# Attention on one core: where the sums of probabilities run, and how many buffers they and the outputs have

## The reference, cut to what matters

```python
def xattn(query, key, value, Wq, Wk, Wv, Wo):           # query (16,112,1024), key = value = ctx (16,375,1024)
    q = (query @ Wq).reshape(b, sq, 32, 32).transpose(0, 2, 1, 3)
    k = (key @ Wk).reshape(b, sk, 8, 32).transpose(0, 2, 1, 3)      # v likewise; each serves 4 heads
    scores = einsum('bhqd,bhkd->bhqk', q, k) * 32 ** -0.5
    probs = softmax(scores, axis=-1)
    out = einsum('bhqk,bhkd->bhqd', probs, v)
    return out.transpose(0, 2, 1, 3).reshape(b, sq, 1024) @ Wo
x = x + xattn(layernorm(x), ctx, ctx, Wq, Wk, Wv, Wo)
x = x + ffn(layernorm(x), w1, w1_scale, w3, w3_scale, w2, w2_scale)  # silu(x w1) * (x w3), then w2
```

## Time and profile before

| | |
|---|---|
| median of 3 runs | 2506.35 us (2501.25 to 2508.3) |
| span of the profiled execution | 2511.5 us (the page gives no other time for it) |
| PE busy | 2424.5 us, 97% of the span, 12682 matmul rows |
| DVE, ACT, POOL busy | 1727.6, 979.1 and 576.1 us |
| line 816, sums | 256 rows, median 563 ns, first at 282.8 us, last at 852.1 us |
| line 924, products with values | 768 rows |

### The profile page before, as it was taken

One profiled execution on the slowest core, in us unless ns is written; L12 is line 12 of the kernel. 1 busy time (PEld: TensorE's weight loads), 2 busy tenths in 40 slices (PEclk: granted clock), 3 DMA queues, 4 the chain that ended last, 5 costly groups with the idle time before them and its releaser, 6 DMA issues.

```text
span 2511.5 us, 35414 instructions
## 1 busy us (share of the span) xinstructions
PE 2424.5 (97%) x12682; PEld 2069.3 (82%) x12682; DVE 1727.6 (69%) x2639; ACT 979.1 (39%) x1673; POOL 576.1 (23%) x305
## 2 busy tenths in 40 slices
PE   7998999999999699799999999999999989999999
PEld 7997878878876388699999988998899978888887
DVE  6425777777776446788888889898889874445442
ACT  3212445444454422444444445344443342323221
POOL 1000354454454400011111111332333320000000
PEclk9998999999998799899999999999999999999999
DMA  7534555455545345465655554666676687565652
GB/s 225 174 96 135 146 135 146 131 142 143 133 113 130 86 155 168 126 203 168 186 170 168 165 151 148 181 180 183 194 211 182 172 284 228 170 186 151 186 163 84
DMA packets 369146, 408.04 MB, mean 162 GB/s; under 512 B 125824, under 2 KB 324096, under 8 KB 359152
## 3 DMA queue, kind: packets, MB, share of 16 engines
q1 hardware_dynamic: 369008, 406.22, 56.7%
HBM read 252.99 MB, written 152.70 MB: 162 GB/s over the span
## 4 chain that ended last, share of the span: by engine, by line
PE 44%; DVE 9%; issue 3%; DMA 2%; ACT 0%; DVEq 0%; ACTq 0%
PE bank L84 15%; PE bank L85 15%; PE bank L86 15%; DVE g_WL L90 2%; DMA stash<-weight_scratch 2%; DVE g_su L1731 1%; DVE stash L1736 1%; DVE g_XL L90 1%; DVE stash L1228 1%; DVE stash L1226 1%; DVE xT L1723 1%; DVE stash L1225 1%; DVE stash L1249 0%; ACT g_XH L1659 0%; ACT g_WH L1198 0%
## 5 line engine op out<-in xcount | busy, mean ns | idle before, releaser
L84 PE MATMUL bank<-g_XH,g_WH 128*128 128x448 f32 (+1 forms) x2254 | 847.1, 376 | 30.2 <-DVE g_XL L90 15.9
L86 PE MATMUL bank<-g_XH,g_WL 128*128 128x448 f32 (+1 forms) x2254 | 845.0, 375 | 0.0
L85 PE MATMUL bank<-g_XL,g_WH 128*128 128x448 f32 (+1 forms) x2254 | 844.9, 375 | 0.0
L84 PEld LDWEIGHTS bank<-g_XH,g_WH 128*128 128x128 f32 x2254 | 424.5, 188 | 93.7 <-DVE g_WL L90 18.1
L86 PEld LDWEIGHTS bank<-g_XH,g_WL 128*128 128x128 f32 x2254 | 424.6, 188 | 55.3
L85 PEld LDWEIGHTS bank<-g_XL,g_WH 128*128 128x128 f32 x2254 | 424.7, 188 | 54.3
L90 DVE TENSOR_TENSOR g_WL<-stash,g_WH 128x512 fp32r<-128x512 f32 (+1 forms) x417 | 349.3, 841 | 75.8 <-ACT g_WH L1198 47.1
L1198 ACT ACTIVATE g_WH<-stash 128x512 fp32r<-128x512 f32 x392 | 241.7, 628 | 398.9 <-PE bank L86 245.1
L696 DVE TENSOR_REDUCE a_nm<-bank 112x1 f32<-112x375 f32 x512 | 264.9, 531 | 117.1 <-PE bank L831 113.8
L800 ACT ACTIVATE a_pr<-bank 125x448 f32<-125x448 f32 x384 | 204.0, 545 | 204.4 <-PE bank L907 150.8
L649 POOL TENSOR_TENSOR a_prsum<-a_pr 125x1792 f32<-125x1792 f32 x32 | 129.3, 4042 | 363.0 <-ACT a_pr L800 363.0
(11 more groups left out here) (132 smaller groups left out, 3617.8 us busy)
## 6 DMA issues: line engine op xcount, KB each, us to landing
stash<-in_L_ffn_w SPq DMA_DIRECT2D x168, 256.0 KB, 5.2
weight_scratch<-stash SPq DMA_DIRECT2D x28, 1024.0 KB, 7.6
stash<-weight_scratch SPq DMA_DIRECT2D x28, 1024.0 KB, 5.4
h_scratch<-g_Sh SPq DMA_DIRECT2D x112, 224.0 KB, 2.8
down_scratch<-xT SPq DMA_DIRECT2D x98, 256.0 KB, 3.0
stash<-in_ctx SPq DMA_DIRECT2D x48, 500.0 KB
stash<-h_scratch SPq DMA_DIRECT2D x25, 896.0 KB, 6.4
a_qst<-q_scratch SPq DMA_DIRECT2D x96, 224.0 KB, 4.7
```

What stands on the lines that cost most here:

```text
L84: pe.matmul(acc, lh, rh, start=first, stop=False, skip_group_check=onto)
L85: pe.matmul(acc, lh, rl, start=False, stop=False, skip_group_check=onto)
L86: return pe.matmul(acc, ll, rh, start=False, stop=last, skip_group_check=onto)
```

## The change

- The sums leave steps 2 and 22. They follow a run of value products: group 1 of the batch before in step 19, group 0 of this batch in step 31, each behind the other group's values.
- They write bank 1, which is one of the two banks of the score products. From head 21 on the parity of the heads' banks is turned (`head_bank`), so that heads 20 and 21 use bank 0 one after the other and bank 1 is free around step 19; likewise heads 31 and 0 around step 31. Heads 1 and 22, the next ones in bank 1, wait for ACT's copy of the sums. The sums wait for the maxima of the heads before.
- `prsum` has two buffers, one per group (the second in `stash`, slots 10 and 11); `o` has two, by the batch's parity (the first in `stash`, slot 7).
- ACT copies the sums and then the output in step 0, and copies sums in step 20 ahead of an exponential.
- The reciprocals of group 0 come in steps 5, 8, 11 and 14 of the next batch, those of group 1 in steps 22, 23, 25 and 27 of it. POOL scales both in the next batch, group 1 ahead of the additions for that batch's group 1.
- On SP's queue the stores of the batch before stand behind the stacks of group 0 and of group 1. After the last body the mixing's first tile waits for the last sums, and the last eighth of Wo is loaded there, after the stores of batch 14, since slots 7, 10 and 11 of `stash` are in use till then.

```diff
-        def load_wo(sp):
+        def load_wo(sp, cs):
...
-                pr, prsum = sb("pr", [P, R, NC, J * SQ]), sb("prsum", [CK, R, J * SQ])
-                o, l = sb("o", [P, NG, J * SQ]), sb("l", [P, NG, J * SQ])
+                pr = sb("pr", [P, R, NC, J * SQ])
+                prsum = (sb("prsum", [CK, R, J * SQ]),
+                         stash[0:CK, 10:12, :].rearrange("p a n -> p (a n)")[:, 0:R * J * SQ]
+                         .rearrange("p (r n) -> p r n", r=R))
+                l = sb("l", [P, NG, J * SQ])
+                o = (stash[:, 7, 0:NG * J * SQ].rearrange("p (g n) -> p g n", g=NG),
+                     sb("o", [P, NG, J * SQ]))
...
-                o_bank = l_bank = bank[6]
+                o_bank, l_bank = bank[6], bank[1]
...
-                SUMS = {2: (1, 1), 22: (0, 0)}
-
-                INV = {25: (0, 0), 27: (0, 1), 28: (0, 2), 31: (0, 3),
-                       5: (1, 0), 8: (1, 1), 11: (1, 2), 14: (1, 3)}
+                SUMS = {19: (1, 1), 31: (0, 0)}
+                assert set(SUMS) == set(PV)
+
+                HEAD_AFTER_SUMS = HEADS[19][-1] + 1
+                assert HEAD_AFTER_SUMS == 21
+
+                INV = {5: (0, 0), 8: (0, 1), 11: (0, 2), 14: (0, 3),
+                       22: (1, 0), 23: (1, 1), 25: (1, 2), 27: (1, 3)}
+
+                def head_bank(h):
+
+                    return s_bank[(h + (h >= HEAD_AFTER_SUMS)) % 2]
...
                         sp.wait_ge(pv_done, NC * NG * (B - 1))
+                        sp.wait_ge(sums_done, NG * B)
                         load_tile(sp, 0)
-                        store(B - 1, 0)
-                        store(B - 1, 1)
+                        for stored in o_stored:
+                            sp.wait_ge(stored, 16 * (B - 1))
+                        load_wo(sp, range(KT - 1, KT))
+                        store(B - 1, 1, 0)
+                        store(B - 1, 1, 1)
...
                                 add(b, 0, 0)
-                                if not (isinstance(b, int) and b == 0):
-                                    scale(b - 1, 1)
+                                if later:
+                                    scale(b - 1, 1 - par, 0)
                                 add(b, 0, 1)
+                                if later:
+                                    scale(b - 1, 1 - par, 1)
                                 add(b, 1, 0)
                                 add(b, 1, 1)
-                                scale(b, 0)
...
-                                if attn and s == 1 and not (isinstance(b, int) and b == 0):
-                                    copy_out(b - 1, 1)
-                                if attn and s - 1 in SUMS:
-                                    g, back = SUMS[s - 1]
-                                    if not (isinstance(b, int) and b < back):
-                                        copy_sums(b - back, g)
+                                if attn and s == 0 and not (isinstance(b, int) and b == 0):
+                                    copy_sums(b - 1, 0)
+                                    copy_out(b - 1, 1 - par, 1)
+                                if attn and s == 20 and not (isinstance(b, int) and b == 0):
+                                    copy_sums(b - 1, 1)
...
-                                    wait(pe, max_done, NH * sb_ + h - 1)
-                                    pe.matmul(s_bank[h % 2][0:SQ, 0:SKP],
+                                    wait(pe, max_done, NH * sb_ + h - (h not in (0, HEAD_AFTER_SUMS)))
+                                    if attn and h == 1:
+
+                                        wait(pe, l_copied, NG * b - 1)
+                                    if attn and h == HEAD_AFTER_SUMS + 1:
+
+                                        wait(pe, l_copied, NG * b)
+                                    pe.matmul(head_bank(h)[0:SQ, 0:SKP],
...
-                                if attn and s in SUMS:
-                                    g, back = SUMS[s]
-                                    if not (isinstance(b, int) and b < back):
-                                        sums(b - back, g)
                                 if attn and s in PV:
 
                                     g = PV[s]
-                                    wait(pe, l_copied, NG * b + g)
+                                    wait(pe, o_copied, NG * b + g)
...
                                         last.then_inc(pv_done, 1)
+                                    sg, back = SUMS[s]
+                                    if not (isinstance(b, int) and b < back):
+
+                                        if score:
+                                            pe.wait_ge(max_done, NH * sb_ + (20 if sg else NH - 1))
+                                        else:
+                                            pe.wait_ge(max_done, NH * (b + 1))
+                                        sums(b - back, sg)
                         each(pe, body)
+                        pe.wait_ge(l_copied, NG * B - 1)
                         sums(B - 1, 1)
```

More of the change, by code:

```diff
@@ L144, in load_ctx @@
                              .rearrange("b k n -> k (b n)")).then_inc(c_loaded[slot], 16)
-        def load_wo(sp):
+        def load_wo(sp, cs):
             rows = wo.rearrange("(g r j d) n -> g j r d n", g=NG, r=R, j=J)
-            for c in range(KT):
+            for c in cs:
                 for r in range(R):
@@ L587, in body @@
                                 sp.wait_ge(v_moved, B)
-                                load_wo(sp)
+                                load_wo(sp, range(KT - 1))
                             if isinstance(b, int) and b == -2:
@@ L600, in body @@
                             if attn and not (isinstance(b, int) and b == 0):
-                                store(b - 1, 1)
+                                store(b - 1, 1 - par, 0)
                             if proj:
                                 load_stacks(i, par, b, 1)
+                            if attn and not (isinstance(b, int) and b == 0):
+                                store(b - 1, 1 - par, 1)
                         def load_stacks(i, par, b, g):
@@ L644, in add, with scale @@
                                 pool.wait_ge(two_added, n + 1)
-                                pool.tensor_tensor(prsum[:], prsum[:], pr[0:CK, :, 2, :], ALU.add
+                                pool.tensor_tensor(acc, acc, pr[0:CK, :, 2, :], ALU.add
                                                    ).then_inc(all_added, 1)
                             else:
-                                wait(pool, sums_done, n)
-                                pool.tensor_tensor(prsum[:], pr[0:CK, :, 0, :], pr[0:CK, :, 1, :],
+                                wait(pool, sums_done, n - 1)
+                                if isinstance(b, int) and b == 0 and g == 1:
+                                    pool.wait_ge(w_lo, KT)
+                                pool.tensor_tensor(acc, pr[0:CK, :, 0, :], pr[0:CK, :, 1, :],
                                                    ALU.add).then_inc(two_added, 1)
-                        def scale(b, g):
+                        def scale(b, par, g):
                             n = NG * b + g
@@ L661, in body @@
                             if attn:
+                                later = not (isinstance(b, int) and b == 0)
                                 add(b, 0, 0)
-                                if not (isinstance(b, int) and b == 0):
-                                    scale(b - 1, 1)
+                                if later:
+                                    scale(b - 1, 1 - par, 0)
                                 add(b, 0, 1)
+                                if later:
+                                    scale(b - 1, 1 - par, 1)
                                 add(b, 1, 0)
                                 add(b, 1, 1)
-                                scale(b, 0)
                         each(pool, body)
-                        scale(B - 1, 1)
+                        scale(B - 1, 1, 0)
+                        scale(B - 1, 1, 1)
                     @block.vector
@@ L729, in body @@
                                                           ).then_inc(v_moved, 1)
[L730 to L735, removed]
+                                if attn and s in INV and not (isinstance(b, int) and b == 0):
+                                    invert(b - 1, *INV[s])
                         each(dve, body)
-                        for j in range(J):
-                            invert(B - 1, 1, j)
+                        for g in range(NG):
+                            for j in range(J):
+                                invert(B - 1, g, j)
                     @block.scalar
@@ L742, in _, with copy_out @@
                         act.wait_ge(wkv_loaded, 32)
-                        def copy_out(b, g):
+                        def copy_out(b, par, g):
                             act.wait_ge(pv_done, NC * (NG * b + g + 1))
```

(7 more changed lines are left out.)

16 lines of the change are left out of this document (8 added, 8 removed).

## The result

The changed kernel takes 2513.64 us (median of 17 runs, 2506.81 to 2519.18) against 2504.18 us (17 runs, 2501.11 to 2512.86) before: the ratio is 1.0031, with a 95% interval of 1.0022 to 1.0041. That is 5.5 to 10.3 us slower. The forecast was 2512.4 us, 6.1 us slower. The time itself came out only 1.2 us off, which is in part luck: the kernel before, put at 2506.35 us for the forecast, has a median of 2504.18 in the 17 runs, so the medians are 9.5 us apart.

The account below looks back on a forecast made before the run. PE's order of issue, and any wait entering it, was taken to bound the attention. Batches 1 to 12 +5.4, batch 0 -0.3, the end +1.0: +6.1 on 2506.35 gives 2512.4 us, range 2498 to 2527.

Parts of the forecast that it names:

- Part 1 and 2: Steps 2 and 22 without sums: -1.48 and -1.07 us; behind value products in steps 19 and 31: +0.75 each.
- N: The moment at which the product of values ends and the next ordinary matmul starts on PE.
- Part 3: Score product 1 waits for ACT's copy of group 0's sums: N + 0.82, not N + 0.29, +0.53 us.
- Part 4: Reciprocals moved to steps 22, 23, 25, 27: score product 26 waits till N + 5.21, +0.97 us per batch.
- The dense batches: Sum of the per-batch terms: +0.45 us per batch, +5.4 us over batches 1 to 12.
- The end: End of stage: POOL's last addition 1 us earlier, mixing tile and Wo's eighth loaded late; +1 us (-1 to +4).
- B: Faster rival: DVE's backlog doesn't reach score product 26, so 11.6 us go: 2500.8 us, chance 0.23.
- C: Slower rival: reciprocals and maxima overlap less, product 31 waits longest, 1.1 us more per batch: 2526 us, chance 0.21.
- D: Slower rival: the two waits pull the granted clock to 1.2 GHz for some 6 us per batch: 2548 us, chance 0.06.
- e7's second rival: The rows of maxima come about 0.3 us later and step 6's transposed scores wait for their DMA.

Follow-up runs that it names:

- e4: e3 with group 0's sums alone in step 2 of the next batch instead of behind step 31's value products; ratio 0.9970.
- e2: Changed kernel with group 0's sums in bank 7, so score product 1 waits for no copy; ratio 1.0023.
- e7: e3 with head 0's maximum taken ahead of the pieces of the negated maxima; ratio 0.9953.
- e3: Changed kernel with group 1's reciprocals in steps 25, 27, 28 and 30 and group 0's sums in bank 7; ratio 0.9975.
- e6: e3 with the step of two score products moved from 24 to 25; ratio 0.9954.
- e1: Changed kernel with group 1's reciprocals moved back to steps 25, 27, 28 and 30; ratio 0.9982.
- e5: e3 with the mixing's attention tile and Wo's last eighth loaded ahead of the wait for the last sums; ratio 0.9959.
- e8: e5, e6 and e7 together; ratio 0.9949 to the kernel before (2494.05 us).

## Why the prediction was right, step by step

- **Part 1 and 2.** Without sums in step 22 product 25 comes 4.17 us behind N (517.13 - 512.96) where it was 5.23: 1.06 less, 1.07 reckoned. Sums inside a value run: 0.76 us for eight passes (3.15 - 2.39), where 0.75 was taken and 1.07 was the upper bound. By the Trainium skill's rule (TensorEngine Tiling (Array Packing), Key Properties), a change of tile within the mode doesn't drain, and the trace agrees, 0.76 against 0.75. The change to another bank, which lies in the same 0.76, shows no price either. e4 gives the other side: alone they cost 0.24 to 0.28 more, 0.32 was reckoned.
- **Part 3.** Product 1 at N + 0.83 for 0.82, product 22 without a wait, N to the transposes of step 3 3.01 for 3.91 - 0.95 = 2.96. The sum held because it let product 2's own 0.24 go when product 1 is late. My expectation for e2 forgot that, and was too large by it: taken away, the wait gave 0.26 to 0.28, and e7 showed the rest at product 2.
- **Part 4.** Product 26 at N + 5.22 for 5.21, and +0.98 from product 25 to the next projection (518.45 - 517.13 = 1.32 in place of 0.34) for 0.97. It is the step that decides the sign. But the reciprocals are guilty of 0.72 of it only (1.32 against 0.60 in e3): without sums in step 22 product 26 comes early enough to meet the maximum of head 24 in any case. Batch 0, which has no reciprocals there, shows it in the changed kernel itself: 13.04 us from step 19 to 31, 0.82 less than the 13.86 before and not 1.07; in e6, with the step moved, it is 12.81.
- **The dense batches.** +0.55 per batch for +0.45: 24.21 - 24.42 = -0.21 up to step 19 (reckoned -0.95 + 0.75 = -0.20), +0.75 behind it (reckoned 0.97 + 0.75 - 1.07 = 0.65). Most of the 0.10 that is left comes after product 26, at product 27 (0.24 us to the next start in place of 0.18), and it goes with the reciprocals in e1, whose 0.81 is these 0.72 and about 0.1 behind them. From the first value run to that of step 31 of batch 12: 473.26 before, 479.04 after, +5.8 for +5.1.
- **The end** was under-sized: from that value run to the mixing's first product 112.26 before, 113.97 after, +1.7 for +1.0. Its size is near by a path that was wrong in two places. POOL's last addition was to release PE 1 us earlier; it did so 0.13 us earlier (858.72 - 757.32 = 101.40 against 852.07 - 750.54 = 101.53). And the landing of the tile was to set the start; the last reciprocals, the scaling and the end of the attention's part set it, after the landing (e5 shows it too), and of the new loads the queued eighth alone adds to it, with its 1.58. That PE's waits for POOL would go and the DMA of the maxima would be next in line is as it was said, though no number was set on it.
- A further 1.0 us of the stage's 8.5 lies ahead of the first value run (74.7 and 75.7 us), where the ten traces spread from 74.2 to 75.7; e1, with the same code there as the changed kernel, has 74.4, so I don't put it down to the change.
- **Rivals.** B falls: DVE's backlog reaches product 26. C falls: behind product 26 no wait enters the table, so the longest one is at 26, not at 31; what comes behind it is the 0.1 us or so at product 27. D falls: the granted clock of the dense stretch is 1.00 with both waits in it. No wait for the DMA of the maxima stands there either.

What stays open: the stretch behind batch 12, with granted clocks of 0.57 to 0.85 from 785 us on in five of the traces, took 109.9 to 114.0 us in the ten traces, and e6 to e8 gave back 1.3 to 2.4 us there. A part of it is e7's second rival: behind batch 12 PE waits 7.3 us in all for the DMA of the maxima in e8, 5.7 in e5. With one profile each I can't say whether the rest is chance or the order of the batches' ends against the clock.

## What to carry to other kernels

Joining two runs of small tiles saves their entry and exit, here about 0.25 us a run; ask at once which buffer the joined work now borrows and what was moved to make room, since two waits of 0.3 and 0.7 us, a batch's 1.04 us with what hangs on them, cost more than both runs gave. On an engine that is 99% busy follow the order of issue of its suppliers: an instruction moved ahead of one that frees a buffer delays the buffer by nearly its whole spacing (0.72 of 0.76 us here), though its engine is idle over a quarter of the time (24.96 of 35 us busy). And take the next wait in line into account when you price the removal of one: the two gave back 0.28 and 0.83 us a batch where 0.54 and 1.06 were expected, because a second, smaller wait stood behind each.

## What the runs showed that I had not expected

Waits of 0.15 to 0.17 us don't show in the table of waits, since matmuls overlap: e3 shows next to none there (0.3 us in all from 270 to 760 us), yet 0.26 and 0.25 us per batch stood behind products 26 and 2, about 0.09 of each as a slower restart (0.26 us to the next start in place of 0.17). They are seen in the distance from start to start, and in a matmul that shows longer than its like.
